# Routed experts' look-ahead and the order of routing, in a fused two-layer attention and mixture-of-experts kernel on one core

## What is computed

```python
x = x + L0_xattn(ctx, ctx, norm(x))   # a long convolution of k*v over 256 channels, times q
x = x + L0_ffn(norm(x))               # 16 experts, each token uses 4, and a shared expert
x = x + L1_xattn(norm(x), ctx, ctx)   # scores over tokens: "bsd,bse->bde", softmax over d
x = x + L1_ffn(norm(x))               # one dense FFN (896 wide) with 8 low-rank experts, 2 per token

# L0_ffn
topk_idx = top 4 of scores + bias, within the best 2 of 4 groups of experts
weight = 2.5 * score / sum of the 4 scores
routed = sum over the 4 experts of weight * (silu(x @ gate.T) * (x @ up.T)) @ down.T
out = routed + silu(x @ sh_gate.T) * (x @ sh_up.T) @ sh_down.T

# L1_ffn
probs = softmax(x @ Wg.T); rw, sel = top 2 of probs; rw = rw / rw.sum()
for k in (0, 1):
    x1 = x @ W1.T + lora1(x, sel[k]); x3 = x @ W3.T + lora3(x, sel[k])
    x2 = silu(x1) * x3
    out += (x2 @ W2.T + lora2(x2, sel[k])) * rw[k]
```

## Time and profile before

| what | us |
| --- | --- |
| median of 3 runs | 835.27 (833.19 to 836.08) |
| the profiled execution | 833.92 |
| its span | 832.2 |
| PE busy in it | 725.8 (87%) |
| DVE, ACT, POOL busy | 539.8, 342.8, 444.2 |

### The profile page before, as it was taken

The page is one execution under the profiler, slowest core; times in us unless marked ns, Lnnn a source line. Parts: engine busy times, 40 slices in busy tenths (PEclk is TensorE's granted clock), DMA queues, the critical chain, the costliest instruction groups (busy, mean ns, idle before and its releaser), DMA issues.

```text
span 832.2 us, 14744 instructions
## 1 busy us (share of the span) xinstructions
PE 725.8 (87%) x5219; PEld 662.9 (80%) x5219; DVE 539.8 (65%) x1278; ACT 342.8 (41%) x702; POOL 444.2 (53%) x534
## 2 busy tenths in 40 slices
PE   4899979847776787945989999999999999999996
PEld 3344567647776776834989999999999999999996
DVE  4999977954443554647777667658666676565533
ACT  2464442233443446535444434443444344433321
POOL 5876936055455554145536646566366565453532
PEclk9999988969998899966999999999999999999999
DMA  7665418755654455244301101002021010000000
GB/s 258 176 177 130 107 54 149 148 97 137 189 151 138 126 156 118 91 156 129 121 1 59 33 13 52 27 27 64 1 59 32 13 40 26 1 14 2 1 14 13
DMA packets 44599, 68.67 MB, mean 83 GB/s; under 512 B 7376, under 2 KB 32240, under 8 KB 44528
## 3 DMA queue, kind: packets, MB, share of 16 engines
q0 software_dynamic: 10080, 28.72, 15.6%
q1 hardware_dynamic: 34352, 38.97, 14.5%
q10 hardware_dynamic: 96, 0.04, 0.0%
HBM read 50.77 MB, written 14.84 MB: 79 GB/s over the span
## 4 chain that ended last, share of the span: by engine, by line
PE 48%; DVE 4%; ACT 2%; POOL 1%; issue 1%; POOLq 0%; DVEq 0%; ACTq 0%
PE psum L1717 17%; PE psum L1702 9%; PE psum L1749 8%; PE psum L1763 4%; PE psum L1735 3%; PE psum L1776 1%; DVE lora_w_lo L2075 1%; PE psum L1787 1%; PE psum L1797 1%; PE psum L1833 1%; PE psum L1813 1%; ACT lora_w_hi L1875 0%; PE psum L1826 0%; POOL rows_back L1989 0%; PE psum L1805 0%
## 5 line engine op out<-in xcount | busy, mean ns | idle before, releaser
L2007 POOL TENSOR_TENSOR hid<-hid,rw_sb 128x256 f32<-128x256 f32 x112 | 93.1, 831 | 153.5 <-DVE hid L2199 153.2
L1717 PE MATMUL psum<-am_hi,lora_w_hi 128*128 128x256 f32 x448 | 127.2, 284 | 2.8 <-DVE am_lo L2194 2.8
L1717 PE MATMUL psum<-am_hi,lora_w_lo 128*128 128x256 f32 x448 | 127.3, 284 | 0.0
L1717 PE MATMUL psum<-am_lo,lora_w_hi 128*128 128x256 f32 x448 | 127.3, 284 | 0.0
L2199 DVE TENSOR_TENSOR hid<-hid,psum 128x256 f32<-128x256 f32 x112 | 46.6, 417 | 116.1 <-ACT hid L1882 116.1
L1182 POOL DMA_INDIRECT rows_in<-y_scratch,slot_token x80 | 78.4, 979 | 68.2 <-DVE row_w L1418 37.6
L1882 ACT ACTIVATE hid<-psum 128x256 f32<-128x256 f32 x112 | 42.6, 383 | 169.1 <-PE psum L1717 167.2
L1717 PEld LDWEIGHTS psum<-am_hi,lora_w_hi 128*128 128x128 f32 x448 | 86.4, 193 | 3.0 <-POOL am_lo L2018 3.0
L2205 DVE TENSOR_TENSOR hid_lo<-hid,hid_hi 128x256 fp32r<-128x256 f32 x112 | 74.6, 686 | 19.6 <-ACT hid_hi L1888 14.5
L1717 PEld LDWEIGHTS psum<-am_hi,lora_w_lo 128*128 128x128 f32 x448 | 86.5, 193 | 0.0
L1717 PEld LDWEIGHTS psum<-am_lo,lora_w_hi 128*128 128x128 f32 x448 | 86.4, 193 | 0.0
(11 more groups left out here) (318 smaller groups left out, 2295.6 us busy)
## 6 DMA issues: line engine op xcount, KB each, us to landing
slots_scratch<-y_out SPq DMA_DIRECT2D x40, 256.0 KB
stage<-in_moe_weights SPq DMA_DIRECT2D x18, 384.0 KB, 3.9
moe_w_lo<-in_moe_weights POOLq DMA_DIRECT2D x18, 384.0 KB, 7.0
lora_stage_early<-in_lora_weights SPq DMA_DIRECT2D x16, 384.0 KB
x_sb<-in_x SPq DMA_DIRECT2D x4, 512.0 KB, 6.1
ctx_t<-in_ctx_t SPq DMA_DIRECT2D x4, 512.0 KB, 7.3
y_scratch<-y SPq DMA_DIRECT2D x8, 256.0 KB, 2.2
ctx_ring<-in_ctx_keys SPq DMA_DIRECT2D x16, 128.0 KB, 2.4
```

The lines of the kernel that those rows point to most:

```text
L1717: last = nc.tensor.matmul(x_banks[F % 2][:, w * GT:(w + 1) * GT], wp, ap, start=False, stop=(half == 1 and k == 2), skip_group_check=True)
L2007: nc.gpsimd.tensor_tensor(f[:, F % 2, k, :], f[:, F % 2, k, :], rw_sb[:, F // FB % 2, k, :], ALU.mult)\
```

## The change

Three parts.

1. **Routed loop.** Rows are turned two steps ahead of gate_up from step 6 on (both 6 and 7 in step 6), and down comes one step later (no down in step 6). So moe_xt has three slots, slot_w three, and there are 45 steps. The hidden turns of odd pairs below 24 go to bank 7, the others to bank 6; from 24 on a hidden turn waits for the low part of the pair before, and bank 7 goes to the first group's scores. w_offset is read behind the first turn.
2. **First group.** Its 8 gathers go behind pairs 21 to 24 and 28 to 31, both tiles into one place, so that those of tile 1 wait on POOL for tile 0's adds. The other parts move by up to 4 steps. The first router's Exp, probs and picks move from the tail's head into step 42; the two masks stay in the tail.
3. **Routing's front and the block's end.** All four slot_tables stand before the last two shared downs. tile_experts works with one tile per partition: 32 elements instead of 64 x 32. A matmul spreads the result over all partitions, between the two last downs; expert_tables reads it from PSUM. tile_hots(3) and tile_experts stand before the last shared products. ACT's copy of group 2 moves behind token_numbers. POOL's add of group 3 moves behind the eighth gather. The odd slot of shared_out lies in the context's ring, so SP loads the six contexts only when x has been added to. POOL has one more affine_select in the front. SP no longer waits for the y stores at the end; POOL and DVE do in the tail.

The diff's core:

```diff
+            def turns_at(n):
+                pairs = (n,) if n < AHEAD_FROM else (n, n + 1) if n == AHEAD_FROM else (n + 1,)
+                return [q for q in pairs if q < ROUTED_PAIRS]
+            def down_at(n):
+                if n == AHEAD_FROM:
+                    return []
+                q = n - 3 if n < AHEAD_FROM else n - 4
+                return [q] if 0 <= q < ROUTED_PAIRS else []
+            def ht_bank(q):
+                return banks[7] if q % 2 and q < ONE_BANK_FROM else banks[6]
...
-                if m == SHARED_STEPS - 1:
-                    slot_table(0)
-                shared_down(m)
-            for block in range(1, HOT_BLOCKS):
+                if m < SHARED_STEPS - DOWNS_LATE:
+                    shared_down(m)
+            for block in range(HOT_BLOCKS):
                 slot_table(block)
+            shared_down(SHARED_STEPS - 2)
+            spread_experts()
+            shared_down(SHARED_STEPS - 1)
...
             def turn_hidden(q):
                 pe.wait_ge(prod_done, of_pairs(q + 1))
-                if q >= 2:
+                if q >= ONE_BANK_FROM:
+                    pe.wait_ge(ht_low, q)
+                elif q >= 2:
                     pe.wait_ge(ht_low, q - 1)
...
             for n in range(STEPS_ROUTED):
-                if n < ROUTED_PAIRS:
-                    turn_rows(n)
-                if 1 <= n <= ROUTED_PAIRS:
-                    gate_up(n - 1)
+                for q in turns_at(n):
+                    turn_rows(q)
+                if n == 0:
+                    pe.wait_ge(offsets_ready, 1)
+                    load_offsets(0)
+                for q in gate_at(n):
+                    gate_up(q)
...
-                if 3 <= n < ROUTED_PAIRS + 3:
-                    down(n - 3)
-                if 2 <= n < ROUTED_PAIRS + 2:
-                    turn_hidden(n - 2)
+                for q in down_at(n):
+                    down(q)
+                for q in hidden_turn_at(n):
+                    turn_hidden(q)
...
-                dve_step(nc.vector.tensor_tensor(reached[:, :, :], tile_nums[:, :].unsqueeze(2).broadcast_to(late),
-                                                 tile_ends[:, :].unsqueeze(1).broadcast_to(late), ALU.is_ge))
-                dve_step(nc.vector.reduce_sum(late_expert[:, :], reached[:, :, :], axis=AX.X))
+                dve_step(nc.vector.tensor_scalar(reached[:, :], tile_ends[:, :], places[:, 0:1], None, ALU.is_le))
+                dve_step(nc.vector.reduce_sum(expert_at[:, :], reached[:, :], axis=AX.X))
...
+                if i == ROW_SLOTS:
+                    add_rows(TOKEN_GROUPS - 1)
...
+                    if t >= 1 and k == 0:
+                        pool.wait_ge(early.added, 3 * t)
                     nc.gpsimd.indirect_dma_start(
-                        out=early.rows_back[:, t, k * DIM:(k + 1) * DIM], out_offset=None,
+                        out=early.rows_back[:, 0, k * DIM:(k + 1) * DIM], out_offset=None,
...
+                if n == PICKS_AT:
+                    first_picks()
...
-            nc.scalar.activation(warm[:, :], minus_half[:, 0:1], ACT.Exp)
-            picks_exp(0)
-            for k in range(STAGE_SLOTS):
-                high_weights(k)
+            high_weights(0)
+            high_weights(1)
             picks_copies(0)
+            high_weights(2)
+            high_weights(3)
...
+            router_picks(0)
             low_weights(0)
             low_weights(1)
-            router_probs(0)
-            router_picks(0)
+            for k in range(Y_SLOTS):
+                dve.wait_ge(early.y_stored[k], 16 * (ROUTED_PAIRS // Y_SLOTS))
+            inputs_product(0, 0)
+            inputs_product(0, 1)
             low_weights(2)
             low_weights(3)
-            inputs_product(0, 0)
-            inputs_product(0, 1)
```

More of the change, by code:

```diff
@@ L677, in __init__, with place @@
             "x_low", "logits_done", "exp_ready", "gate_loaded", "step"))
-    def place(self, sb):
+        self.probs_exp, self.order_made = map(sem, ("probs_exp", "order_made"))
+        self.y_stored = [sem(f"y_stored{i}") for i in range(Y_SLOTS)]
+    def place(self, nc, sb):
         T = TILES
+        with nc.sbuf_tensor("first_rows_place", [P, TOP_EXPERTS * DIM], FP32):
+            with nc.sbuf_tensor("moe_xt_hi_more", [P, GROUP_T], F32R) as more_hi:
+                with nc.sbuf_tensor("moe_xt_lo_more", [P, GROUP_T], F32R) as more_lo:
+                    self.xt_more = more_hi, more_lo
         self.rows_back = sb("rows_back", [P, ROW_TILES, TOP_EXPERTS * DIM])
@@ L721, in moe_phase @@
         pass
-    with nc.sbuf_tensor("reached", [P, LATE_TILES, 2 * E], FP32) as reached:
-        pass
     ht_hi, ht_lo = (sb(n, [P, 2, h_cols], F32R) for n in ("ht_hi", "ht_lo"))
@@ L845, in _ @@
                   .then_inc(y_stored[q % Y_SLOTS], 16)
-            for i in range(Y_SLOTS):
-                sp.wait_ge(y_stored[i], 16 * (ROUTED_PAIRS // Y_SLOTS))
             for i in range(2):
@@ L1140, in _ @@
                     first_input_copies()
+                if n == PROBS_AT:
+                    act_eng.wait_ge(early.exp_ready, 1)
+                    nc.scalar.activation(early.probs[:, :, :], early.probs[:, :, :], ACT.Exp).then_inc(early.probs_exp, 1)
         @block.gpsimd
@@ L1167, in _ @@
             last.then_inc(order_done, 1)
+            pool.wait_ge(order_done, 4)
+            nc.gpsimd.affine_select(out=first_places[:, :], in_=first_places[:, :], compare_op=ALU.is_gt, fill=0.0,
+                                    base=E, pattern=[[0, 1]], channel_multiplier=-1).then_inc(order_done, 1)
             for k in range(LOWS_EARLY, FBLOCKS):
@@ L1446, in first_add @@
             def first_add(t):
-                rows, half = early.rows_back[:, t, :], 2 * DIM
+                rows, half = early.rows_back[:, 0, :], 2 * DIM
                 dve.wait_ge(early.gathered[t], 16 * TOP_EXPERTS)
@@ L1538, in _, with lora_probs, lora_picks @@
                     first_shift()
-    return lora_stage
+                if n == PICKS_AT:
+                    first_picks()
+    return lora_stage
+def lora_probs(nc, early, step):
+    probs, prob_sum = early.probs[:, :, :], early.prob_sum[:, :]
+    step(nc.vector.reduce_sum(prob_sum, probs, axis=AX.X))
+    step(nc.vector.reciprocal(prob_sum, prob_sum))
+    step(nc.vector.tensor_tensor(probs, probs, prob_sum.unsqueeze(2).broadcast_to([P, TG, LORA_EXPERTS]), ALU.mult))
+def lora_picks(nc, early, step):
+    wide, prob_sum, top = [P, TG, LORA_EXPERTS], early.prob_sum[:, :], early.top
+    for k in range(PICKS):
+        pick_first_max(step, nc, early.probs[:, :, :], wide, early.order[:, :].unsqueeze(1).broadcast_to(wide),
+                       (top[:, k, :], early.hit[:, k, :, :], early.top_hit[:, :]))
+    step(nc.vector.tensor_tensor(prob_sum, top[:, 0, :], top[:, 1, :], ALU.add))
+    step(nc.vector.reciprocal(prob_sum, prob_sum))
+    step(nc.vector.tensor_tensor(early.rw[:, :, :].rearrange("p t k -> p k t"), top[:, :, :],
+                                 prob_sum.unsqueeze(1).broadcast_to([P, PICKS, TG]), ALU.mult))
 def lora_unit(a, k):
@@ L2061, in _ @@
         def _(dve):
-            steps = [1]
+            steps = [1 + 18]
             def dve_step(ins):
```

227 lines of the change are left out of this document (125 added, 102 removed).

## The result

The changed kernel takes 831.52 us (median of 20 runs, 828.87 to 834.25); the kernel before, beside it, 834.0 (829.93 to 838.15). The ratio is 0.997, 95% interval 0.9958 to 0.9983: 2.5 us faster, where 17.4 were forecast. The profiled execution has a span of 828.0, 4.2 under the one of before.

What follows compares the result with a forecast made beforehand. The prediction took PE's late signs during GpSimd's gathers to bound the routed loop. Gains of 11.8 (loop), 2.2 (front) and 3.4 (block end, tail head) summed to 17.4: 816.5 profiled, 817.9 as median, range 796 to 831 us.

Steps and rivals of the forecast that it cites:

- What bounds the kernel: Routed loop: PE's done-signs reach ACT 1.9 to 2.5 us late during GpSimd's gathers, closing a two-pair cycle of 7.44 us.
- The routed loop: gate_up(6) to gate_up(36): more PE cover lets cycles take three pairs; 129.65 becomes 117.9 us, 11.8 gained.
- 0, and 1 us if they are late: First group on POOL: cost of tile 1's gathers waiting there for tile 0's three adds, with later row gathers queued behind.
- The cycle's formula: Routed loop: period is 2.5 k + 2.4 us for bursts of k pairs; 3.7 per pair at k = 2, 3.3 at 3.
- PE's down on ht_lo under 15: Sign of being right, routed loop: PE's wait there falls from 28.8 us to under 15.
- Front: Routing's front: gathers' chain ends last and starts earlier, the rest follows at its old distance; 2.2 us gained, bounds 0 to 4.
- Block end and head: Block end and tail head: 18 DVE steps 3.8, barrier 1.2; 0.3 gained at the boundary, 3.1 in the tail, 3.4 together.
- That stretch stays: Last 402 us, PE busy 395.4: nothing of the change lies there, so no gain or loss.
- D: Rival: waits only change names, front and tail hide behind POOL, time within 0.3% (2.5 us); chance 0.07.
- C: Rival: slower, 842.5 (median 843.9), stalls of about 4 us per cycle, ten cycles, granted clock under 0.8; chance 0.06.
- A: Rival: look-ahead hides all lateness, 796.3; marks are 96 us for the loop and no POOL wait for row_w; chance 0.20.
- B: Rival: GpSimd's cycle sets the pace, 826.8; mark is bursts of four gathers at 7.4 us; chance 0.18.

Runs made afterwards that it cites:

- run 4: Changed kernel, row gathers on POOL replaced by plain DMAs on SP, rows in order (routed result differs): 790.58 us, ratio 0.9466 to the kernel before.
- run 7: Changed kernel, POOL making the tail's first low input between gathers of batches 2 and 3: 799.1 us, ratio 1.0079 to the kernel before (793.61 there).
- run 1: Changed kernel, first group's rstd moved behind pairs 29 and 36, tile 1's gathers behind 29 to 32: 826.88 us, ratio 0.9883 to the kernel before.
- run 12: Changed kernel with the first group's rstd and tile 1's gathers later on POOL, on another occasion: 824.97 us, ratio 0.9905 to the kernel before.
- run 2: Changed kernel with the look-ahead alone undone: 836.1 us, ratio 0.9988 to the kernel before.
- run 11: Changed kernel without the look-ahead alone, on another occasion: 831.83 us, ratio 0.999 to the kernel before.
- run 13: Changed kernel with look-ahead, third xt slot and first group's new places undone; front, second bank and picks stay: 828.49 us, ratio 0.9935 to the kernel before.
- run 5: Changed kernel, first group's rstd and tile 1's gathers later, POOL held back one pair: 797.83 us, ratio 1.006 to the kernel before (793.61 there).
- run 18: Changed kernel without look-ahead and first group's new places, with POOL held back one pair and 32 unused bytes: 827.75 us, ratio 0.9862 to the kernel before.
- second trace of the changed kernel: The changed kernel itself, unedited, traced again on another occasion: 832.21 us, ratio 0.999 to the kernel before.
- run 6: Changed kernel with two 128x2048 operations put back on DVE between tile experts and last shared product: 797.9 us, ratio 1.0068 to the kernel before.
- second pair: Kernel before and changed kernel, both unedited, measured again on another occasion: 833.68 and 832.21 us, changed kernel's ratio 0.999.
- run 16: Changed kernel with the first group's router Exp, probs and picks back in the tail's head: 833.74 us, ratio 0.9991 to the kernel before.
- run 14: Changed kernel with 32 unused bytes ahead of hid_hi in the tail: 830.65 us, ratio 0.9942 to the kernel before.
- run 17: Kernel before with 128 unused bytes ahead of hid_hi: 836.72 us, ratio 0.9991 to the kernel before.

## Why the prediction was wrong

**What bounds the kernel: right, and now shown** by run 4, but only where signs are late (run 7). By the rule that the prediction takes from the Trainium skill ("Perfetto Trace Analysis", section "Tensor Engine Instruction (MATMUL, LD_WEIGHTS)"), a late sign would be late work. What is shown is narrower: PE makes a pair in 2.93 once POOL issues no row gathers. Whether under gathers the work or only its sign is late, no run here separates.

**The routed loop: the step that failed** is "0, and 1 us if they are late" for the first group on POOL. I priced only tile 1's gathers, which wait for tile 0's adds, and gave no thought to the rstd behind pair 27, on the same queue: a term put at nothing. It moved a pair forward while what it needs moved back, and POOL runs four pairs ahead of PE. POOL's stop of 6.9 there, and the burst of 14 that followed, cost 3.6 and 4.5 us between gate_up(26) and (36), 4.4 and 6.7 between (6) and (36), and some 7 of the median (the changed kernel against runs 1 and 12, which move rstd and tile 1's gathers together). That is about half of the 10.3 by which the loop fell short. Runs 2 and 11 (51.4 and 50.6, without look-ahead) and run 13 (44.7) put the loss on the first group's new places; up to 3.8 of it is the three rows_back gathers that now fall into this stretch. The 1.9 behind pair 36 is not the stop's: (36) to (39) takes 10.9 in runs 1, 4, 5 and 12 too, and 9.0 in runs 13 and 18, where the first group's later steps stand as before. That long bursts make long lateness was in my formula, but I let bursts grow to three pairs only.

**The cycle's formula** held about: bursts of six gathers came at 10.3, 10.3 and 10.9 in the second trace of the changed kernel (9.9 forecast). But POOL did not stay at k = 3, and this is the second term that was mis-sized: gate_up(6) to (26) gained 7.2, where the forecast's prices give some 12 (15 x 3.3 + 3 x 4.55 + 4.85 + 3.6, and 2 for the rest, 73.6). The 15 is right by the forecast's own places; its sum counts 13, 9, 4 and 4 pairs at 3.3, 3.6, 4.55 and 4.85 (112.9), where its places give 15, 7, 3 and 5 (112.6). With the stop gone, the loop's 30 pairs take 123.8 and 122.8 (runs 1 and 12), not 117.9. And of the 7.2 the order has little. Without it this stretch took 79.2 and 78.5 (runs 2 and 11), in run 13, with the second bank but two xt slots and the old places, 84.95. Run 13 issues all 8 rows_back gathers ahead of gate_up(26), and 5 ahead of (20); runs 2 and 11 issue 5 and 3. At 1.25 each this makes some 3.8 of the 5.7 to 6.4, and 2.5 of the 2.0 to 2.8 that lie ahead of pair 20; what is left for the third slot, 2 to 2.7 in all, no run shows by itself. Look-ahead itself, run against run, is worth 0.000 to 0.002 of the time (at most 0.003 by the medians), but both pairs of runs have a stop at rstd in them (6.9 and 7.9 with look-ahead, 3.4 and 3.3 without). What look-ahead brings without the stop was not run by itself.

So the sign "PE's down on ht_lo under 15" came in one trace (11.9) and not in the other (17.4), and one sign of being wrong came near: PE's waits kept their sum, though only 3.6 of the 33.4 are at its turns of rows.

**Front: mis-sized in our favour.** The gathers' chain ended last, as said, and began at 171.4, as said. "The rest follows at its old distance" was the fault: the old distance held gathers stretched by DVE's wide operations (run 6). 4.5 and, in the second pair, 3.7 instead of 2.2.

**Block end and head.** The steps' 3.8 was right; the "barrier 1.2" was not. From DVE's last step to the tail it is 3.7, and run 16 shows that the block ends as late without those steps. Run 13 has both the picks and a short end (8.1 from the last transpose to the first cast, 10.5 in the changed kernel). What ends the block is POOL's instruction DRAIN at the barrier, as the view of POOL's last line shows it (duration in ns, then first and last start), in the changed kernel and in run 4:

```profile
L796 POOLq DRAIN  x1: 9333/9333/9333, 346.1 to 346.1; - x1
...
L796 POOLq DRAIN  x1: 3210/3210/3210, 310.5 to 310.5; - x1
```

In the changed kernel it ends at 355.48, and the tail starts at 355.74; DVE was through at 352.35. It begins with POOL's last operation, first_x_lo of the first group, and takes 9.31 to 9.34 in every trace here but run 4's, where the rows are not on POOL and it takes 3.21. first_x_lo starts 3.3 behind gate_up(39) before (3.2 in run 13) and 4.7 in the changed kernel, without look-ahead too (runs 2 and 11). So the end belongs to the first group's later steps, and neither to the picks nor to look-ahead. The prediction priced DVE's steps and a barrier of 1.2, and not this drain. What the drain waits for, no run shows. POOL's eight gathers are indeed next late, and they took what DVE had given. 0.6 (0.7 in the second pair) instead of 3.4.

**"That stretch stays"**: it lost 1.9. 0.2 in each group, some 1.4 in all, comes from where the new buffers put hid and t (runs 14 and 17). A last piece, some 0.9, is a stretch at half clock (1.2 GHz) in the last 5 to 6 us: the last two groups take 111.0 and 111.2 with it, 110.3 in run 1 without it. Both traces of the changed kernel have it and the two of the kernel before have not. It goes with neither kernel, though: run 17, the kernel before but for 128 bytes, has it (from 829.2), and runs 1 and 13 have not. Its cause stays open.

**Rivals.** D had the closest time, and its "the waits only change their names" fits PE's sum of waits. But that came of parts that cancel: the front's gain did not hide behind POOL, and the stop on POOL, which D doesn't have, took it back. C's point was never reached: the 10-us stall did come, with the granted clock at 0.72 in it, but once and not in ten cycles. A's and B's marks did not come either: POOL waited 18.1 for row_w, and the bursts were uneven, from 1 to 14. (Of the forecast's own bounds, 812 should read 813.5: 835.3 less 11.8, 4 and 6.)

## What to carry to other kernels

An engine that issues gathers runs pairs ahead; everything on its queue that waits for another engine has to be placed by that lead, and moved when either side moves. A stop there costs twice, once as starved rows and once as the burst behind it. Before a gain is booked to a reordering, list every wait on every queue that it shifts, and run the change's parts one by one: here the front gained 4, the stop on POOL cost some 7, the moved buffers 1, and the whole came out at 1 to 2.5. And before two stretches of a loop are compared, count what each of them holds: a gain of 7.2 was by half a move of work across the border. A changed allocation can cost in code that nobody touched.

## What was not expected of the hardware

- While POOL issued row gathers, ACT started up to 10.4 us behind the profile's (modelled) end of the PE work that it waited for, and nothing in the trace names another cause: on four occasions, and in no trace of a fifth. The kernel before took 833 to 837 on the four and 793.6 on the other.
- Gathers on POOL took 1.97 to 2.41 instead of 0.95 where they started beside a 128x2048 DVE operation (run 6, and the first one before), and 1.11 where one started 0.30 ahead of it.
- Moving hid and t by 32 or 128 bytes changed a group's time of 55.60 or 55.40 to 55.20, with no instruction changed. By the sizes of what is allocated ahead of them (each rounded up to 32 bytes), they begin 96 bytes behind their old place in the changed kernel, and 128 behind it in runs 14 and 17. No trace shows an address, and which property of it counts was not tried.
